# One load of the recurrence's weights for both sequences, and one turn of the output weights' sign

## The chip, the cores and the metric

The kernel runs on one core of one Trainium2 chip. Its engines are TensorE (PE, matrix products; PEld is its loading of weights), VectorE (DVE), ScalarE (ACT), GpSimd (POOL) and SyncE (SP), which here only issues transfers. The metric is the device time of one execution in microseconds. A profiled execution lies beside the timed ones.

## The reference, cut to what matters

Four layers are computed for two sequences of 512 tokens and 256 channels (attention and experts, a state space with a spline MLP, a linear recurrence with a table MLP, attention and experts). The change touches the third. Its first half is a linear recurrent unit with 32 complex states, kept as 64 real rows (real parts, then imaginary parts):

```
u_t  = B x_t                       B: 64 x 256, real rows and imaginary rows
h_t  = lambda * h_(t-1) + gamma * u_t      complex, by state
y_t  = C_re Re(h_t) - C_im Im(h_t) + D * x_t
```

The minus sign is why the imaginary half of the output weights is turned. The second half is a gated MLP whose weights come from a table of 16 values. Its products are independent of the recurrence, and both are added to the sequence.

## The kernel before, in words

Every layer is a block in which each engine runs its own list of instructions, and the blocks are separated by a barrier of all engines (`run`). One block holds one layer for one sequence. In the recurrence's blocks the sequences are worked on one after the other, sequence 0 and then sequence 1; `linear_recurrence(m, b, ..., split_here)` writes the lists, and `split_here` is true for sequence 0 only.

At the start of a block SP issues three transfers (L2597 to L2599): the input weights `w_b`, the output weights `w_c` and the skip weights `skip`. TensorE clears its accumulators with two small products (L2560, `clear_acc`), waits for `w_b` and `w_c`, and projects the normed input `xnT` by four products into a PSUM bank (L2605). VectorE waits for the loads and the projection, turns the sign of the lower half of `w_c` (L2648), and scales the projection into `h` (L2649). The recurrence over 512 tokens is then done by nine doublings: TensorE multiplies a shifted `h` by a power of lambda (L2612), VectorE adds the product to `h` (L2655). The first doubling stands ahead of the first table product; the other eight stand between the table MLP's items. The MLP's products go through a helper (L225). At the end `h` is multiplied by `w_c` into the accumulators (L2640).

For sequence 0 only, ScalarE rounds the table weights in three pieces (L2673) and GpSimd subtracts to get the low parts (L2692); TensorE waits for the first piece ahead of the first table product, for the second (the down weights) at item 1, and for the third ahead of item 4 of eight. In both sequences GpSimd then waits for `skip`, multiplies it by the normed input (`extra`, L2696) and adds that to the sequence (L2699). The join at the end of the block (L2729) adds the accumulators to the sequence, after GpSimd's two steps. The norm of the other sequence runs inside the block as well, in eight phases spread over the items (lines 588 to 659), and must not write `xn` before `extra` was made.

Of the kernel before, what the change touches and what calls it, by code (L numbers as in the profile page):

```python
# [28 lines left out]
FP32 = mybir.dt.float32  # L29
# [4 lines left out]
ALU = mybir.AluOpType  # L34
AXIS = mybir.AxisListType

P = 128
BATCH, T, D = 2, 512, 256
NT = T // P
# [2523 lines left out]

def linear_recurrence(m, b, ctx, parts, norm, split_here):

# [7 lines left out]
    sb = m.local(ctx)  # L2573
    w_b, w_c = sb("w_b", [P, KD, N2]), sb("w_c", [N2, D])
    h = sb("h", [N2, T])
# [3 lines left out]
    piece_high, piece_split = m.sig("lut_high"), m.sig("lut_split")  # L2579
    extra, skip = sb("extra", [P, NT, D]), sb("skip", [P, D])  # L2580
    skip_loaded, skip_step = m.sig("skip_loaded"), m.sig("skip_step")
# [14 lines left out]
    def sync(sp):  # L2596
        sp.dma_start(w_b[:], dram["lru_b"]).then_inc(loaded.sem, 16)  # L2597
        sp.dma_start(w_c[:], dram["lru_c"]).then_inc(loaded.sem, 16)
        sp.dma_start(skip[:], dram["lru_d"].broadcast_to([P, D])).then_inc(skip_loaded.sem, 16)  # L2599

    def tensor(pe):
        clear_acc(m, pe)
        pe.wait_ge(loaded.sem, loaded.at(32))
        for k in range(KD):
# [39 lines left out]
    def vector(dve):  # L2644
        dve.wait_ge(loaded.sem, loaded.at(32))
        dve.wait_ge(projected.sem, projected.at(1))

        nc.vector.tensor_scalar(w_c[STATES:], w_c[STATES:], -1.0, None, ALU.mult)  # L2648
        nc.vector.tensor_scalar(h[:], lru_psum, m.lru_gamma[:], None, ALU.mult).then_inc(h_ready.sem, 1)  # L2649

        def double(s):
            dve.wait_ge(h_ready.sem, h_ready.at(s + 1))
            dve.wait_ge(stepped.sem, stepped.at(s + 1))
            shift = 1 << s
            nc.vector.tensor_tensor(h[:, shift:], h[:, shift:], lru_psum[:, shift:], ALU.add)\  # L2655
              .then_inc(h_ready.sem, 1)

        double(0)
        gate(dve, 0, None, 0, 0)
        for n in range(ITEMS):  # L2660
            if n < NT:
                double(2 * n + 1)
                double(2 * n + 2)
            if n + 1 < ITEMS:
                gate(dve, n + 1, None, (n + 1) % NT, (n + 1) % 2)
            store_low(dve, n, n % 2)
            for phase in norm_phases(n):
                norm.vector(dve, phase)
# [18 lines left out]
    def gpsimd(pool):  # L2687
# [6 lines left out]

        pool.wait_ge(skip_loaded.sem, skip_loaded.at(16))
        nc.gpsimd.tensor_tensor(extra[:], m.xn[:], skip[:].unsqueeze(1).broadcast_to([P, NT, D]), ALU.mult)\  # L2696
# [4 lines left out]
    def close():  # L2701
        mlp.close()
        norm.close()
        if split_here:
            piece_high.close(3)
            piece_split.close(3)
        loaded.close(32)
        skip_loaded.close(16)
        skip_step.close(2)
        for s, n in ((projected, 1), (h_ready, STEPS + 1), (stepped, STEPS)):  # L2710
            s.close(n)
# [61 lines left out]
def hybrid_stack_kernel(nc, dram, out):  # L2773
    with ExitStack() as ctx:
# [32 lines left out]
        with ExitStack() as late_ctx:  # L2807
            m.hold_parts(late_ctx)
            with ExitStack() as parts_ctx:
                parts = [parts_ctx.enter_context(nc.sbuf_tensor(f"lut_{part}", [P, LUT_COLS], FP32R))  # L2810
                         for part in ("high", "low")]
                for b in range(BATCH):
                    with ExitStack() as layer_ctx:
                        m.turn_to(b)
                        skip_step = m.sig("skip_step")
                        norm = Norm(m, 1 - b, 2 + b, (5, 5), (skip_step.sem, skip_step.at(1)))
                        recurrence, done = linear_recurrence(m, b, layer_ctx, parts, norm, b == 0)
                        run(m, recurrence, join(m, b, done, (skip_step, 2)))
# [151 lines left out]
```

## Time and profile before

| what | us |
|---|---|
| median of 3 runs | 1654.25 |
| their range | 1653.96 to 1656.31 |
| the profiled execution | 1653.79 |
| its span, first to last instruction | 1651.9 |
| TensorE busy | 1528.8 (93%) |
| VectorE busy | 1148.0 (69%) |
| ScalarE busy | 952.4 (58%) |
| GpSimd busy | 703.5 (43%) |

Times in the rows are microseconds from the span's start unless ns is written. The mean granted clock of TensorE in the profiled execution is 0.979 of full speed. The recurrence's two blocks lie at about 977.9 to 1031.4 (sequence 0) and 1031.4 to 1080.8 (sequence 1). An idle time in square brackets stands before the instruction that ended it, with what released it.

### The profile page before, as it was taken

What the parts mean: (1) busy time and instruction counts of PE and PEld (TensorE: products, weight loads), DVE (VectorE), ACT (ScalarE), POOL (GpSimd) and SP (SyncE); (2) the same over time, 40 slices, a digit from 0 to 9 for tenths busy, and PEclk for the clock granted to TensorE, in tenths of its full rate; (3) what the DMA queues carried; (4) which work ended last, traced back from release to release, by engine and by line L of the source; (5) the groups of instructions that cost most, each with busy time, mean ns of one, the idle gap of its engine ahead of it and who ended that gap; (6) DMA issues with size and microseconds to landing.
All of it is one profiled execution on the core that took longest, in us unless ns stands there. A gap on an engine that the chain in (4) does not pass through costs nothing. (4 is left out here: it accounts for less than half of the span.)

```text
span 1651.9 us, 26447 instructions
## 1 busy us (share of the span) xinstructions
PE 1528.8 (93%) x8400; PEld 1208.0 (73%) x8400; DVE 1148.0 (69%) x2620; ACT 952.4 (58%) x2076; POOL 703.5 (43%) x686
## 2 busy tenths in 40 slices
PE   5999989979999998899989989879999997999998
PEld 4777779957787998555635547668888885888887
DVE  5887866558888667799889964446666444666733
ACT  5767656846666566666476533246666444665643
POOL 4999953323222233099639860121223222212222
PEclk9999999989999999999999999979999998999999
DMA  4212222111112121240050000011121112112121
GB/s 124 90 54 81 76 97 96 37 56 36 51 41 93 65 96 58 55 179 1 1 202 32 0 7 1 7 52 50 35 89 39 58 38 72 42 51 73 39 73 36
DMA packets 34334, 98.38 MB, mean 60 GB/s; under 512 B 6388, under 2 KB 11256, under 8 KB 32072
## 3 DMA queue, kind: packets, MB, share of 16 engines
q1 hardware_dynamic: 33064, 90.95, 16.5%
q0 software_dynamic: 1184, 6.37, 1.1%
q8 instruction: 44, 0.72, 0.2%
q14 instruction: 42, 0.34, 0.1%
HBM read 96.12 MB, written 1.18 MB: 59 GB/s over the span
## 5 line engine op out<-in xcount | busy, mean ns | idle before, releaser
L921 POOL TENSOR_TENSOR head_low<-head,head_high 128x512 fp32r<-128x512 f32 x64 | 81.6, 1276 | 453.3 <-ACT head_high L911 452.5
L1953 POOL TENSOR_TENSOR experts_low<-experts,experts_high 128x1024 fp32r<-128x1024 f32 (+3 forms) x62 | 138.9, 2243 | 256.5 <-ACT experts_high L1904 93.2
L2508 POOL TENSOR_TENSOR rings<-du,bc_rows 128x512 f32<-128x512 f32 x124 | 155.6, 1276 | 21.3 <-DMA bc_rows<-bc_rows 14.7
L1309 ACT ACTIVATE probs<-banks,neg_max 128x512 f32<-128x512 f32 (+3 forms) x256 | 133.6, 525 | 53.2 <-DVE neg_max L1192 47.7
L2434 DVE TENSOR_TENSOR_SCAN banks<-banks,rings 128x512 f32<-128x512 f32 x128 | 155.9, 1219 | 3.3 <-POOL rings L2508 2.3
L1586 DVE SCALAR_TENSOR_TENSOR hidden<-banks,weight,act_out 128x96 f32<-128x96 f32 (+1 forms) x192 | 62.7, 367 | 124.2 <-ACT act_out L1554 124.1
L1554 ACT ACTIVATE act_out<-banks 128x256 f32<-128x256 f32 (+2 forms) x112 | 47.4, 423 | 164.9 <-PE banks L225 164.7
L2226 PE MATMUL banks<-rings,ident 128*128 128x512 f32 x256 | 126.4, 607 | 16.6 <-DVE rings L2457 16.3
L225 PE MATMUL banks<-experts_high,xnT_high 128*128 128x384 f32 (+1 forms) x384 | 139.1, 362 | 0.8 <-PEq L187 0.8
L225 PE MATMUL banks<-xnT_high,head_high 128*128 128x512 f32 x256 | 109.9, 429 | 30.1 <-POOL head_low L921 23.5
L225 PE MATMUL banks<-experts_high,xnT_low 128*128 128x384 f32 (+1 forms) x384 | 137.2, 357 | 0.0
L225 PE MATMUL banks<-experts_low,xnT_high 128*128 128x384 f32 (+1 forms) x384 | 137.1, 357 | 0.0
L2332 ACT ACTIVATE banks<-delta,A 128x512 f32<-128x512 f32 x128 | 88.5, 692 | 72.3 <-DVE rings L2457 72.2
L1212 DVE TENSOR_REDUCE row_max<-banks 128x1 f32<-128x512 f32 (+3 forms) x256 | 117.4, 484 | 6.4 <-PE banks L1020 6.1
L1324 ACT ACTIVATE probsT<-banks 128x384 f32<-128x384 f32 (+3 forms) x192 | 87.4, 528 | 47.8 <-PE banks L1029 47.6
L225 PE MATMUL banks<-xnT_low,head_high 128*128 128x512 f32 x256 | 103.7, 405 | 0.0
L225 PE MATMUL banks<-xnT_high,head_low 128*128 128x512 f32 x256 | 103.5, 404 | 0.0
L1205 DVE TENSOR_SCALAR probs<-probs,row_inv 128x512 f32<-128x512 f32 (+3 forms) x240 | 98.1, 448 | 4.8 <-DVE row_inv L1198 0.3
L1162 DVE TENSOR_TENSOR w_in<-banks,w_in 32x512 f32<-32x512 f32 x128 | 87.2, 681 | 13.2 <-DMA w_in<-in_rope_sin 9.1
L2226 PEld LDWEIGHTS banks<-rings,ident 128*128 128x128 f32 x256 | 45.3, 191 | 68.2 <-DVE rings L2457 38.2
L1029 PE MATMUL banks<-ident,probs 128*128 128x128 f32 x640 | 82.2, 276 | 12.5 <-DVE probs L1205 12.3
L2457 DVE TENSOR_TENSOR rings<-banks,bc_rows 128x512 f32<-128x512 f32 x128 | 85.9, 672 | 0.0
(305 smaller groups left out, 4699.1 us busy)
## 6 DMA issues: line engine op xcount, KB each, us to landing
head<-in_heads SPq DMA_DIRECT2D x64, 384.0 KB, 3.1
experts<-in_experts SPq DMA_DIRECT2D x16, 1152.0 KB, 5.2
bc_rows<-bc_rows SPq DMA_DIRECT2D x30, 512.0 KB, 5.8
experts<-in_experts SPq DMA_DIRECT2D x16, 768.0 KB, 4.3
values<-in_values SPq DMA_DIRECT2D x32, 256.0 KB, 3.2
coef<-in_spline_coef POOLq DMA_DIRECT2D x8, 768.0 KB, 4.7
idx<-in_lut_idx SPq DMA_DIRECT2D x16, 134.0 KB, 2.1
x<-in_x SPq DMA_DIRECT2D x2, 512.0 KB, 4.5
```

Of the source, the lines that this page charges most:

```text
L225: last = nc.tensor.matmul(out, left[a], right[b], start=start and n == 0, stop=stop and n == 2, **kw)
L1162: chain.link(nc.vector.tensor_tensor(rot[to:to + 32, which], qk_psum[of:of + 32, which], rope_sin[of:of + 32], ALU.mult))
L1205: last = nc.vector.tensor_scalar(prob_tile(i), prob_tile(i), row_inv[:, i:i + 1], None, ALU.mult)
L1212: last = nc.vector.reduce_max(row_max[:, i:i + 1], score_tile(i), AXIS.X)
L1309: last = nc.scalar.activation(prob_tile(i), score_tile(i), ACT.Exp, bias=neg_max[:, i:i + 1], scale=QK_SCALE, accum_out=row_sum[:, i:i + 1])
L1324: nc.scalar.activation(probsT[:, at:at + cols], m.banks[:, k, 0:cols], ACT.Copy)\
L1953: nc.gpsimd.tensor_tensor(parts[gpar][1][:, columns], raw[gpar][:, columns], parts[gpar][0][:, columns].bitcast(FP32), ALU.subtract)\
L2226: nc.tensor.matmul(y_psum(c), m.ident[:], product[:, step % PRODUCTS], start=n == 0, stop=n == NS - 1)\
L2332: nc.scalar.activation(state_psum(step), delta[:, c], ACT.Exp, scale=A[:, c, n:n + 1])\
L2434: nc.vector.tensor_tensor_scan(state_psum(step), state_psum(step), inflow[:, step % INFLOWS], 0.0, ALU.mult, ALU.add).then_inc(scanned.sem, 1)
L2457: nc.vector.tensor_tensor(product[:, step % PRODUCTS], state_psum(step), C_of(n), ALU.mult)\
L2508: nc.gpsimd.tensor_tensor(inflow[:, step % INFLOWS], du[:, c], B_of(n), ALU.mult)\
```

## The change

The three weights become tiles that live over both blocks. Their transfers, TensorE's wait for them, GpSimd's wait for `skip`, and the turn of the sign are made for sequence 0 only. In sequence 0 the turn moves ahead of VectorE's wait for the projection.

```diff
-def linear_recurrence(m, b, ctx, parts, norm, split_here):
+def linear_recurrence(m, b, ctx, parts, weights, norm, split_here):
...
-    w_b, w_c = sb("w_b", [P, KD, N2]), sb("w_c", [N2, D])
+    w_b, w_c, skip = weights
...
-    extra, skip = sb("extra", [P, NT, D]), sb("skip", [P, D])
+    extra = sb("extra", [P, NT, D])
...
     def sync(sp):
-        sp.dma_start(w_b[:], dram["lru_b"]).then_inc(loaded.sem, 16)
-        sp.dma_start(w_c[:], dram["lru_c"]).then_inc(loaded.sem, 16)
-        sp.dma_start(skip[:], dram["lru_d"].broadcast_to([P, D])).then_inc(skip_loaded.sem, 16)
+        if split_here:
+            sp.dma_start(w_b[:], dram["lru_b"]).then_inc(loaded.sem, 16)
+            sp.dma_start(w_c[:], dram["lru_c"]).then_inc(loaded.sem, 16)
+            sp.dma_start(skip[:], dram["lru_d"].broadcast_to([P, D])).then_inc(skip_loaded.sem, 16)
 
     def tensor(pe):
         clear_acc(m, pe)
-        pe.wait_ge(loaded.sem, loaded.at(32))
+        if split_here:
+            pe.wait_ge(loaded.sem, loaded.at(32))
...
     def vector(dve):
-        dve.wait_ge(loaded.sem, loaded.at(32))
+        if split_here:
+
+            dve.wait_ge(loaded.sem, loaded.at(32))
+            nc.vector.tensor_scalar(w_c[STATES:], w_c[STATES:], -1.0, None, ALU.mult)
         dve.wait_ge(projected.sem, projected.at(1))
-
-        nc.vector.tensor_scalar(w_c[STATES:], w_c[STATES:], -1.0, None, ALU.mult)
         nc.vector.tensor_scalar(h[:], lru_psum, m.lru_gamma[:], None, ALU.mult).then_inc(h_ready.sem, 1)
...
-        pool.wait_ge(skip_loaded.sem, skip_loaded.at(16))
+        if split_here:
+            pool.wait_ge(skip_loaded.sem, skip_loaded.at(16))
...
-        loaded.close(32)
-        skip_loaded.close(16)
+            loaded.close(32)
+            skip_loaded.close(16)
...
+                weights = [parts_ctx.enter_context(nc.sbuf_tensor(f"lru_{name}", shape, FP32))
+                           for name, shape in (("b", [P, KD, 2 * STATES]), ("c", [2 * STATES, D]), ("skip", [P, D]))]
```

## Rows read from the trace of the kernel before

**Rows 1.** The page, part 1, and the granted clock in 40 slices of part 2

```profile
PE 1528.8 (93%) x8400; PEld 1208.0 (73%) x8400; DVE 1148.0 (69%) x2620; ACT 952.4 (58%) x2076; POOL 703.5 (43%) x686
...
PEclk9999999989999999999999999979999998999999
```

**Rows 2.** Windows: length, busy time (instructions) by engine, clock, DMA share, GB/s

```profile
977.90:1031.40 53.50, 46.18 (x232) 32.76 (x232) 23.21 (x57) 17.76 (x35) 14.30 (x5) 0.90 0.02 6
1031.40:1080.80 49.40, 43.25 (x232) 31.01 (x232) 22.29 (x61) 12.51 (x31) 4.75 (x2) 0.97 0.02 6
```

**Rows 3.** Waits from 977.9 to 1080: total us, times, longest

```profile
PE banks L2612 <- DVE h L2649: 4.6, 2, 3.1
...
PE banks L2605 <- DMA w_c<-in_lru_c: 3.9, 2, 2.0
```

**Rows 4.** Order in time on GpSimd: start, duration, instruction, idle before

```profile
979.39 3.10 POOL L2692 TENSOR_TENSOR lut_low<-lut_w,lut_high 128x1376 fp32r<-128x1376 f32 x1 [13.69 <-ACT lut_high L2673]
...
979.39 6.48 POOL L2692 TENSOR_TENSOR lut_low<-lut_w,lut_high 128x1376 fp32r<-128x1376 f32 x2 [13.69 <-ACT lut_high L2673]
...
1035.53 2.40 POOL L2696 TENSOR_TENSOR extra<-xn,skip 128x1024 f32<-128x1024 f32 x1 [41.76 <-DMA skip<-in_lru_d]
```

**Rows 5.** Order in time on TensorE, start of sequence 1

```profile
1031.48 0.59 PE L2560 MATMUL acc<-mask_bf,ident_bf 1*128 1x512 bf16 x2 [1.64 <-PEq L187]
1034.05 3.32 PE L2605 MATMUL banks<-xnT,w_b 128*64 128x512 f32 x4 [1.98 <-DMA w_c<-in_lru_c]
1038.88 1.07 PE L2612 MATMUL banks<-h,lru_step 64*64 64x511 f32 x2 [1.51 <-DVE h L2649]
...
1042.96 0.43 PE L225 MATMUL banks<-lut_high,xnT_high 128*128 128x344 f32 x1
```

**Rows 6.** Order in time on VectorE, start of sequence 1

```profile
1037.48 0.59 DVE L2648 TENSOR_SCALAR w_c<-w_c 32x256 f32<-32x256 f32 x1 [6.32 <-PE banks L2605]
1038.09 0.74 DVE L2649 TENSOR_SCALAR h<-banks,lru_gamma 64x512 f32<-64x512 f32 x1
```

**Rows 7.** Windows of 1 us; the clock is the third number from the end

```profile
987.00:988.00 1.00, 1.00 (x2) 0.12 (x2) 0.00 (x0) 0.00 (x0) 1.00 (x1) 0.50 0.00 0
...
994.00:995.00 1.00, 1.00 (x8) 1.00 (x8) 0.68 (x1) 0.00 (x0) 0.00 (x0) 1.00 0.00 0
...
1034.00:1035.00 1.00, 0.95 (x2) 0.42 (x3) 0.00 (x0) 0.00 (x0) 0.00 (x0) 0.72 0.28 92
1035.00:1036.00 1.00, 1.00 (x2) 0.23 (x1) 0.00 (x0) 0.00 (x0) 0.47 (x1) 0.50 0.02 7
...
1038.00:1039.00 1.00, 0.12 (x1) 0.12 (x2) 0.81 (x2) 0.00 (x0) 0.99 (x1) 1.00 0.00 0
```

**Rows 8.** Order in time on TensorE: four fp32 products of another stage

```profile
847.62 1.12 PE L2137 MATMUL banks<-xmT,w_in 128*128 128x512 f32 x2 [0.20 <-DVE delta L2413]
848.58 1.02 PE L2137 MATMUL banks<-xn,w_in 128*128 128x512 f32 x2
```

**Rows 9.** Order in time on TensorE, start of sequence 0

```profile
980.50 3.27 PE L2605 MATMUL banks<-xnT,w_b 128*64 128x512 f32 x4 [1.92 <-DMA w_c<-in_lru_c]
986.84 1.96 PE L2612 MATMUL banks<-h,lru_step 64*64 64x511 f32 x2 [3.07 <-DVE h L2649]
...
993.95 0.43 PE L225 MATMUL banks<-lut_high,xnT_high 128*128 128x344 f32 x1
```

**Rows 10.** Order in time on VectorE, start of sequence 0

```profile
983.88 2.14 DVE L2648 TENSOR_SCALAR w_c<-w_c 32x256 f32<-32x256 f32 x1 [6.21 <-PE banks L2605]
986.04 0.74 DVE L2649 TENSOR_SCALAR h<-banks,lru_gamma 64x512 f32<-64x512 f32 x1
```

**Rows 11.** Instructions on the tile `h`: duration ns min/median/max, first and last start

```profile
L2655 DVE TENSOR_TENSOR h<-h,banks x18: 411/661/679, 988.9 to 1062.7; 64x511 f32<-64x511 f32 x2, 64x510 f32<-64x510 f32 x2, 64x508 f32<-64x508 f32 x2, 64x504 f32<-64x504 f32 x2
```

**Rows 12.** Windows of 1 us in the attention stage; the three between show 0.50

```profile
1095.00:1096.00 1.00, 1.00 (x6) 0.56 (x5) 0.00 (x0) 0.00 (x0) 0.00 (x0) 0.94 0.00 0
...
1099.00:1100.00 1.00, 1.00 (x7) 0.73 (x7) 1.00 (x5) 0.97 (x1) 0.00 (x0) 0.85 0.00 0
```

More of the change, by code:

```diff
@@ L2816, in hybrid_stack_kernel @@
                         norm = Norm(m, 1 - b, 2 + b, (5, 5), (skip_step.sem, skip_step.at(1)))
-                        recurrence, done = linear_recurrence(m, b, layer_ctx, parts, norm, b == 0)
+                        recurrence, done = linear_recurrence(m, b, layer_ctx, parts, weights, norm, b == 0)
                         run(m, recurrence, join(m, b, done, (skip_step, 2)))
```

## The prediction, made before the changed kernel was built

> **What bounds the kernel now.** TensorE is busy for 93% of the span, so I read its stalls first and ask of every other engine only whether TensorE waits for it [rows 1]. The whole-kernel chain of waits is of little use here: it is followed back from the end and never reaches the recurrence. So I took the two stages of the recurrence by themselves. The window view gives 53.50 us for sequence 0 and 49.40 us for sequence 1, at a mean granted clock of 0.90 and 0.97, where the page's row of the clock shows 9s but for three slices [rows 1, 2]. Both stages run the same products on TensorE (232 each), so the reader should already ask why one is 4 us longer and why the clock is low in both. The view of waits between 977.9 and 1080 names what belongs to the change: TensorE waits 3.9 us in two pieces for the transfer of `w_c` (the projection, L2605), and 4.6 us in two pieces for `h` (L2612 after L2649) [rows 3]. GpSimd waits 41.76 us for `skip`, across most of a stage, but nobody waits for GpSimd there [rows 4]. The rest comes from the order in time on TensorE, VectorE and GpSimd at the start of each stage, and from the granted clock microsecond by microsecond.
>
> **Sequence 1, the transfers.** TensorE issues the two small products that clear the accumulators at 1031.48; they end at 1032.07. The projection starts at 1034.05, with 1.98 us of idle time ended by the DMA of `w_c` [rows 5]. The change takes out the three transfers and the wait, and its input `xnT` was finished in the stage before, so the four products can follow the two directly: 1.98 us, all of it on the path, since everything after hangs on the projection. On SP nothing is queued behind the three issues in this stage, so their removal there is worth nothing by itself.
>
> **Sequence 1, the sign.** The projection ends at 1034.05 + 3.32 = 1037.37. VectorE turns the sign of `w_c` from 1037.48 and starts `h` at 1038.09; without the turn `h` can start at 1037.48: 0.61 us, on the path, for TensorE's first doubling waits for `h` [rows 5, 6].
>
> **Sequence 1, the clock.** The four projection products take 3.32 us here [rows 5]. The granted clock tells why: it is 0.72 in the microsecond from 1034 and 0.50 in the one from 1035, that is 1.2 instead of 2.4 GHz, and full again from 1038 [rows 7]. Between 1029.84, the end of the last stage's products (the start at 1031.48 less its idle 1.64), and 1034.05 TensorE had done nothing but the 0.59 us pair. Four products of 128x512 in fp32 at the full clock take 1.98 us in another stage, from 847.62 to 848.58 + 1.02 = 849.60 [rows 8]. If the transfer's gap goes, the projection starts after 1.64 us of idle and the pair, about 0.1 us of overlap aside, and I expect it to run and end before any drop: 3.32 - 1.98 = 1.34 us. The bound on one side is 0 (the drop comes all the same; it can't cost more, since it is there now), on the other 1.34. I take 1.34, since the gap that precedes the drop is cut from 3.62 us of idle in 4.21 to 1.64 in 2.23. Sum for sequence 1: 1.98 + 0.61 + 1.34 = 3.93 us.
>
> **Sequence 0, the sign.** Here the transfers stay, and TensorE's wait for them (1.92 us) stays too [rows 9]. But the turn moves ahead of VectorE's wait for the projection. Before, it starts at 983.88, the projection having ended at 980.50 + 3.27 = 983.77, and takes 2.14 us for 32x256 elements, against 0.59 us in sequence 1; `h` starts at 986.04 [rows 6, 10]. What is different is GpSimd. Its first two subtractions of table weights run from 979.39 to 982.49 and on to 985.87; the turn that started inside the second ends 986.02, that is 0.15 us after it. In sequence 1 GpSimd's `extra` ends at 1035.53 + 2.40 = 1037.93 and the turn at 1038.07, again 0.14 after it [rows 4, 6, 10]. So the turn is held to the end of the GpSimd instruction that it meets, and alone costs some 0.15 us. After the change VectorE can turn when `w_c` has landed, about 980.50, inside GpSimd's first piece; it should end at 982.49 + 0.15 = 982.64, which is 1.13 us before the projection's end. `h` then starts at 983.88: 2.16 us, on the path. The cover is that 1.13 us; if it were gone, the turn would show again on VectorE ahead of `h`. The wait that moves has only the turn queued behind it, and TensorE's own wait for the same 32 already ends no earlier.
>
> The Trainium skill, SBUF — State Buffer, "Who interferes with whom", says that a VectorE instruction in a two-port mode and a GpSimd instruction exclude each other for a whole instruction, whichever comes second being blocked. By that rule the turn ends behind the first piece, and the trace agrees (2.14 us against 0.59 us for the same work) [rows 6, 10].
>
> **Sequence 0, the clock.** TensorE does nothing from 983.77 to 986.84, 3.07 us, and the granted clock is 0.50 in the microsecond from 987 and full again only from 994 [rows 7, 9]. In sequence 1 the same gap is 1.51 us (1037.37 to 1038.88) and the clock stays full behind it [rows 5, 7]. After the change the gap is 1.51 - 0.61 = 0.90 us in both. The price is read from the same instructions at both clocks: from the first doubling, over twelve table products and the second doubling, to the next table product it is 993.95 - 986.84 = 7.11 us here and 1042.96 - 1038.88 = 4.08 us in sequence 1. The difference is 3.03 us [rows 5, 9]. Bounds 0 and 3.03; I take 3.03, since the new gap is shorter than the one that did no harm. Sum for sequence 0: 2.16 + 3.03 = 5.19 us.
>
> **What comes late next.** In sequence 0 the first doubling ends at 986.84 + 1.96 = 988.80; moved by 2.16 and run at the full clock (1.0 us instead of 1.96) it lets the first table product start near 985.7, which needs GpSimd's first piece, ready at 982.49; the down weights (985.87) are wanted behind the third table product and the last piece (985.87 + 3.1, about 989) ahead of the fifth, both later than that even when moved. GpSimd's use of `skip` in sequence 1 moves from 1035.53 to the start of the stage, about 1031.5, and nobody waits [rows 4]; held back again it would still cost nothing, for it is used at the join only. The VectorE additions into `h`, which now run beside other GpSimd work than before, took 0.661 us in the median and 0.679 at most over both stages, so none of them was held up [rows 11]. The same 9.12 us therefore passes on to the stages that follow, which hang on these through a barrier of all engines. The three tiles kept longer are memory, not time: 0, by bounds 0 and 0.
>
> **The sum.** 5.19 + 3.93 = 9.12 us. The profiled execution took 1653.79 us (span 1651.9), 0.46 under the median of 1654.25; from the median, 1654.25 - 9.12 = 1645.13. I forecast 1645.1.
>
> **The rivals.**
> A. The clock does not come back. The transfers and the turn leave the path as above, but a low stretch still falls on the first products of one or both sequences, or falls in a later stage instead. For it: the clock also fell near 1095.9 while TensorE was busy for the whole of that microsecond, so idle time isn't all of it [rows 12]. Against: the new gaps are shorter than the 1.51 us that did nothing. With none of the clock's gain the change is worth 2.16 + 1.98 + 0.61 = 4.75, giving 1649.5; with only the sequence 1 term lost, 1646.5; with only sequence 0's lost, 1648.2. Chance 0.25.
> The Trainium skill, TensorE: Matmul & The Clock Gate, Part 1, says that the monitor's window runs free of the kernel's start, so that the point of a change varies from run to run. By that rule the moment of each drop against the work is a matter of chance, which is rival A; the one trace shown can't tell.
> B. The turn loses its race and is held to the end of GpSimd's second piece (985.87) as now. Then `h` in sequence 0 starts at 986.04, the gap of 3.07 us and the low clock stay, and only 3.93 remains: 1650.3. For it: GpSimd's pieces follow each other without a gap [rows 4]. Against: before, the turn got in at the seam between second and third. Chance 0.05.
> C. The three transfers were hidden anyway: something else holds the projection of sequence 1 to 1034.05. For it: the DMA is only the last that ended. Against: GpSimd's wait of 41.76 us ends with a transfer of the same three [rows 4], and the projection has no other fresh input. Then 5.19 + 0.61 = 5.80, giving 1648.5. Chance 0.04.
> D. Slower. In the attention stage behind, the clock fell near 1095.9 with TensorE busy, for five rows (0.94, three of 0.50, 0.85), which costs 0.06 + 1.50 + 0.15 = 1.71 us of full clock [rows 12]. That dense stage and its twin start 9 us earlier after the change, and the moments of such drops could fall on more of their work. The change is slower than before from six additional ones (10.3 us against 9.12), and by over 0.2% (3.3 us) from eight: 1645.1 + 13.7 = 1658.8. Against: the page's row of the clock shows 9s in all slices of those stages but two [rows 1]. Chance 0.02.
>
> **How the numbers follow.** Forecast 0.64, A 0.25, B 0.05, C 0.04, D 0.02. The range reaches up to A's and nearly B's time, 1650.0, and down to where the low clock under sequence 0's projection goes as well (3.27 - 1.98 = 1.29) and one stretch like D's less in a later stage (1.71): 1645.1 - 3.0 = 1642.1; I take 1642.0. A measurement of this kernel can tell about 0.2%, 3.3 us, from no change, so "same" is 1650.9 to 1657.6. The forecast and rivals B and C lie below it, narrowly for B; giving half of B and a seventh of A to "same" by scatter of the runs makes 0.06. Faster 0.92, same 0.06, slower 0.02.
>
> **What would show it.** In the profile after: one issue each of `w_b`, `w_c` and `skip`; the projection of sequence 1 directly behind the clearing pair, idle near 0, four products in about 2.0 us; the turn once, starting near 980.5 and ended by 982.7, before the projection ends; `h` in sequence 0 starting 0.1 us behind the projection and TensorE's gap there 0.9 us; the granted clock 1.00 through both doublings and the first table products. Stage lengths should be near 48.3 and 45.5 us. The prediction is wrong if the turn ends after 983.8, if the clock is 0.50 in either place, or if the attention stage behind takes more low clock than before.

## The result, and the profile after

The changed kernel takes 1645.15 us in the median of 20 runs (1640.40 to 1653.06), the kernel before 1654.11 us in the median of 20 runs beside it (1649.08 to 1663.19). The ratio is 0.9945 with a 95% interval of 0.9931 to 0.9958: faster by 0.55%, some 9 us, which is clear of the 0.2% that can be told. The profiled execution took 1643.16 us with a span of 1641.6. By the interval the gain is between 6.9 and 11.4 us. Single executions of either kernel lie over 12 us apart, so one profile of each says where a wait went, and the means over the runs say how much it was worth.

The page, beside [rows 1], and the windows of the two sequences, beside [rows 2]:

```profile
PE 1524.4 (93%) x8400; PEld 1205.3 (73%) x8400; DVE 1148.1 (70%) x2619; ACT 952.4 (58%) x2076; POOL 703.1 (43%) x686
...
PEclk9999999989999999999999999989999998999999
```

```profile
976.20:1024.70 48.50, 43.45 (x232) 30.96 (x232) 23.22 (x57) 17.76 (x35) 14.34 (x5) 0.96 0.02 6
1024.70:1073.20 48.50, 44.51 (x232) 32.33 (x232) 21.75 (x60) 12.52 (x31) 4.72 (x2) 0.93 0.00 1
```

The first window is the whole of sequence 0: from clearing product to clearing product it is 1024.76 - 976.22 = 48.54 us, where it was 53.49 before. The clock rose there from 0.90 to 0.96. In sequence 1 it fell from 0.97 to 0.93, and the gain of that sequence is small in this one execution. Sequence 1 is best measured from its clearing product to the attention's first product. These are the first clearing product and the attention's first product of the kernel before, and then of the changed kernel:

```profile
977.99 0.59 PE L2560 MATMUL acc<-mask_bf,ident_bf 1*128 1x512 bf16 x2 [1.64 <-PEq L187]
1086.41 0.80 PE L225 MATMUL banks<-xnT_high,head_high 128*128 128x512 f32 x1 [6.89 <-POOL head_low L921]
976.22 0.59 PE L2560 MATMUL acc<-mask_bf,ident_bf 1*128 1x512 bf16 x2 [1.64 <-PEq L187]
1078.34 0.80 PE L225 MATMUL banks<-xnT_high,head_high 128*128 128x512 f32 x1 [6.94 <-POOL head_low L921]
```

With the clearing products of sequence 1 at 1031.48 and 1024.76, sequence 1 took 54.93 us before and takes 53.58 us here: 1.35 us less, where the sum has 3.93.

TensorE's order in time, sequence 0 and then sequence 1 (start, duration, instruction, idle before), which answers to [rows 9] and [rows 5]:

```profile
978.75 3.58 PE L2607 MATMUL banks<-xnT,lru_b 128*64 128x512 f32 x4 [1.93 <-DMA lru_c<-in_lru_c]
983.16 1.07 PE L2614 MATMUL banks<-h,lru_step 64*64 64x511 f32 x2 [0.84 <-DVE h L2652]
987.23 0.42 PE L225 MATMUL banks<-lut_high,xnT_high 128*128 128x344 f32 x1
...
1024.76 0.59 PE L2560 MATMUL acc<-mask_bf,ident_bf 1*128 1x512 bf16 x2 [1.65 <-PEq L187]
1025.28 2.35 PE L2607 MATMUL banks<-xnT,lru_b 128*64 128x512 f32 x4
1028.46 1.96 PE L2614 MATMUL banks<-h,lru_step 64*64 64x511 f32 x2 [0.84 <-DVE h L2652]
...
1034.84 0.43 PE L225 MATMUL banks<-lut_high,xnT_high 128*128 128x344 f32 x1
```

The gap ahead of the first doubling is 0.84 us in both, down from 3.07 and 1.51. The projection of sequence 1 follows the clearing pair (the two small products that clear the accumulators) without a gap. From the first doubling to the first table product behind the second one, sequence 0 takes 987.23 - 983.16 = 4.07 us, where it took 7.11; sequence 1 takes 1034.84 - 1028.46 = 6.38, where it took 4.08. VectorE and GpSimd, beside [rows 10], [rows 6] and [rows 4]:

```profile
978.73 2.15 DVE L2650 TENSOR_SCALAR lru_c<-lru_c 32x256 f32<-32x256 f32 x1 [2.82 <-DMA lru_c<-in_lru_c]
982.37 0.74 DVE L2652 TENSOR_SCALAR h<-banks,lru_gamma 64x512 f32<-64x512 f32 x1 [1.49 <-PE banks L2607]
...
1027.66 0.74 DVE L2652 TENSOR_SCALAR h<-banks,lru_gamma 64x512 f32<-64x512 f32 x1 [3.22 <-PE banks L2607]
```

```profile
977.63 3.10 POOL L2695 TENSOR_TENSOR lut_low<-lut_w,lut_high 128x1376 fp32r<-128x1376 f32 x1 [13.69 <-ACT lut_high L2676]
...
1024.74 2.38 POOL L2700 TENSOR_TENSOR extra<-xn,lru_skip 128x1024 f32<-128x1024 f32 x1 [32.70 <-SPq L187]
```

The turn still takes 2.15 us, but it starts when the weights land, ends at 980.88, which is 0.15 us behind GpSimd's first piece (980.73), and lies wholly under the projection. GpSimd uses `skip` at the very start of sequence 1. The clock in single microseconds, beside [rows 7]:

```profile
982.00:983.00 1.00, 0.33 (x1) 0.00 (x0) 0.64 (x1) 0.00 (x0) 1.00 (x1) 0.85 0.00 0
983.00:984.00 1.00, 0.84 (x2) 0.19 (x2) 0.11 (x1) 0.00 (x0) 1.00 (x1) 1.00 0.00 0
...
1028.00:1029.00 1.00, 0.54 (x1) 0.29 (x2) 0.41 (x1) 0.00 (x0) 1.00 (x1) 0.50 0.00 0
```

In sequence 0 the clock is full from the first doubling on, as forecast. In sequence 1 it went to half during the projection, 1.9 us after TensorE had taken up work, and stayed there for 6.8 us (1026.7 to 1033.5), over the first doubling and most of the twelve table products.

### The profile page after: what moved, and what is told of

The parts are those of the page before. It is cut to its first block and busy times, and to the rows that moved or that the text cites. A ratio compares the mean times of both kernels' runs of the same rounds, so it can differ in the third digit from the quotient of the medians.

```text
span 1641.6 us, 26441 instructions
## 1 busy us (share of the span) xinstructions
PE 1524.4 (93%) x8400; PEld 1205.3 (73%) x8400; DVE 1148.1 (70%) x2619; ACT 952.4 (58%) x2076; POOL 703.1 (43%) x686
```

## The experiments

Two theories stood against each other. The first is the sum of the prediction: a path of 4.75 us (waiting, turning) and a clock that the shorter gaps give back. The rival says that the clock's drops fall where they will, so that only the path is earned. A second question is what held the turn for 2.14 us.

**The changed kernel again, each part alone, and GpSimd out of the way.** Four kernels on one chip; the kernel before took 1656.53 us there (29 runs).

The changed kernel unedited:

> The changed kernel itself, as the yardstick of the three others on this chip. By my sum it is 9.1 us faster than the kernel before (a ratio of 0.9945). In its trace the turn of the sign ends near 0.15 us behind GpSimd's first subtraction, and TensorE's gap ahead of the first doubling is 0.84 us in both sequences. The rival that takes the clock for a matter of chance expects the two low stretches of the recurrence at other places than in the first trace after the change (979 to 982 and 1026 to 1033), and a time anywhere from 1640 to 1653.

Measured: 1647.06 us (6 runs), ratio 0.9932 (0.9909 to 0.9955). The turn, the gap of 0.84 us and the 48.32 us of sequence 0 came back. Sequence 1 met a low stretch of 13.7 us (1025.7 to 1039.3). TensorE's first two doublings there, and the clock beside them:

```profile
1028.34 1.96 PE L2614 MATMUL banks<-h,lru_step 64*64 64x511 f32 x2 [0.84 <-DVE h L2652]
1033.97 1.96 PE L2614 MATMUL banks<-h,lru_step 64*64 64x510 f32 x2
```

```profile
1030.00:1031.00 1.00, 1.00 (x4) 0.77 (x4) 0.59 (x1) 0.00 (x0) 0.00 (x0) 0.50 0.00 0
1039.00:1040.00 1.00, 1.00 (x5) 0.41 (x3) 0.00 (x0) 0.40 (x1) 0.00 (x0) 0.84 0.00 0
```

Both doublings take 1.96 us, the mark of the half clock, and TensorE is busy for the whole of the microseconds shown. Sequence 1 takes 58.16 us in this profile, 3.2 us more than before the change, 1.5 us of it a longer wait for GpSimd's first step of the attention (8.41 us against 6.89 before). So the short gap does not protect the sequence in every execution.

Loads once, the turn of sequence 0 left in its old place (against the changed kernel):

```diff
             dve.wait_ge(loaded.sem, loaded.at(32))
+        dve.wait_ge(projected.sem, projected.at(1))
+        if split_here:
             nc.vector.tensor_scalar(w_c[STATES:], w_c[STATES:], -1.0, None, ALU.mult)
-        dve.wait_ge(projected.sem, projected.at(1))
```

> The transfers and waits of sequence 1 are gone and the sign is turned once, but in sequence 0 the turn stays behind VectorE's wait for the projection. My sum: only sequence 1's 3.93 us are left (1.98 of waiting, 0.61 of turning, up to 1.34 of clock), so 1650.2, 5.2 us slower than the changed kernel. In the trace the turn of sequence 0 takes about 2.1 us and ends 0.15 us behind GpSimd's second subtraction; TensorE's gap there is 3.07 us. If the clock's part of sequence 0 is not real, it is only 2.2 us slower than the changed kernel.

Measured: 1649.73 us (12 runs), ratio 0.9964 (0.9946 to 0.9982), 6.0 us faster than before (3.0 to 8.9 by the interval), where the sum has 3.93. The turn and TensorE at the start of both sequences:

```profile
984.76 1.90 DVE L2652 TENSOR_SCALAR lru_c<-lru_c 32x256 f32<-32x256 f32 x1 [6.46 <-PE banks L2607]
...
987.48 1.27 PE L2614 MATMUL banks<-h,lru_step 64*64 64x511 f32 x2 [2.82 <-DVE h L2653]
...
1031.16 1.93 PE L2607 MATMUL banks<-xnT,lru_b 128*64 128x512 f32 x4
1033.92 1.07 PE L2614 MATMUL banks<-h,lru_step 64*64 64x511 f32 x2 [0.84 <-DVE h L2653]
```

The turn ends at 986.66; GpSimd's second piece ended at 986.52, 0.14 us before. Sequence 1 is what I had predicted for it: the projection takes 1.93 us at the full clock, and the stretch from its clearing pair to the attention's first product is 50.84 us, where it was 1086.41 - 1031.48 = 54.93 before. That is 4.09 us against 3.93 in the sum.

The turn moved in sequence 0, all else as before (against the kernel before):

```diff
-        dve.wait_ge(projected.sem, projected.at(1))
-
-        nc.vector.tensor_scalar(w_c[STATES:], w_c[STATES:], -1.0, None, ALU.mult)
+        if split_here:
+            nc.vector.tensor_scalar(w_c[STATES:], w_c[STATES:], -1.0, None, ALU.mult)
+        dve.wait_ge(projected.sem, projected.at(1))
+        if not split_here:
+            nc.vector.tensor_scalar(w_c[STATES:], w_c[STATES:], -1.0, None, ALU.mult)
```

> The kernel before with one line moved: in sequence 0 the turn stands ahead of the wait for the projection. Transfers, waits and the second turn stay in sequence 1. My sum: 5.19 us faster than before (2.16 of path and 3.03 of clock), 1649.1. Without the clock's part 2.2 us faster, 1652.1. In the trace the gap of TensorE ahead of the first doubling is about 0.85 us in sequence 0 and 1.51 us in sequence 1.

Measured: 1651.96 us (12 runs), ratio 0.9970 (0.9954 to 0.9987), 5.0 us faster than before (2.2 to 7.6 by the interval), against 5.19 in the sum and 2.2 without the clock, which lies at the very edge of the interval: the times alone do not exclude it. In this profile sequence 0 takes 48.28 us, 5.21 less than before, with a gap of 0.84 us. In sequence 1 the gap is 1.35 us, and the low clock lasted 10.2 us there instead of 3.4. The two parts alone give 0.36% and 0.30%, together 0.66%, and the whole change on the same chip 0.68%: they add, as far as intervals of that width can tell.

GpSimd held back while VectorE turns, the turn itself unmoved (against the kernel before):

```diff
             at = slice(*pieces[piece])
-
+            if n == 1:
+                pool.wait_ge(h_ready.sem, h_ready.at(1))
...
+        pool.wait_ge(h_ready.sem, h_ready.at(1))
         pool.wait_ge(skip_loaded.sem, skip_loaded.at(16))
```

> The kernel before with the turn where it was, but GpSimd waits for h ahead of its second subtraction in sequence 0 and ahead of the use of skip in sequence 1, so that it is idle while VectorE turns the sign. If the turn is held only by the GpSimd instruction that it meets, it takes some 0.15 to 0.3 us in both sequences instead of 2.14 and 0.59, h starts 2.0 and 0.4 us earlier, and the kernel is 2.4 to 5.4 us faster than before (the upper end with the clock's 3.03 us of sequence 0). If GpSimd has nothing to do with it, the turn takes 2.14 and 0.59 us as before and the time is that of before.

Measured: 1652.25 us (12 runs), ratio 0.9970 (0.9952 to 0.9989), 5.0 us faster than before. The turn in sequence 0 and in sequence 1:

```profile
984.23 0.28 DVE L2648 TENSOR_SCALAR w_c<-w_c 32x256 f32<-32x256 f32 x1 [6.48 <-PE banks L2605]
...
1034.85 0.28 DVE L2648 TENSOR_SCALAR w_c<-w_c 32x256 f32<-32x256 f32 x1 [7.72 <-PE banks L2605]
```

With no GpSimd instruction running it takes 0.28 us in both places, against 2.14 and 0.59 before. So 1.86 and 0.31 us of it were waiting for GpSimd. TensorE's gap ahead of the first doubling is 1.21 us in both sequences, and the clock is full behind it. This is the experiment that settles the turn: the same instruction at the same place, and only GpSimd moved. The Trainium skill, SBUF — State Buffer, "Who interferes with whom", calls this an exclusive lock for the whole instruction; the runs agree, with ends 0.14 to 0.15 us behind GpSimd's.

**What else could be earned, and what the terms hang on.** Four kernels on another chip, where the kernel before took 1657.46 us (16 runs).

A step of the turn's size back in sequence 1, in front of `h` (this edit and the next three are against the changed kernel):

```diff
         dve.wait_ge(projected.sem, projected.at(1))
+        if not split_here:
+            nc.vector.tensor_scalar(w_c[STATES:], w_c[STATES:], 1.0, None, ALU.mult)
```

> The changed kernel with a second step on the output weights in sequence 1, a multiplication by 1.0 of the same 32x256 elements behind the wait for the projection, where the turn stood. Nothing holds GpSimd back any more, so its addition to x now runs from about 1027.2 to 1029.6 of the first trace after the change, and the step would begin at 1027.66 inside it. If VectorE is held to the end of the GpSimd instruction that it meets, the step takes 1.9 to 2.1 us instead of the 0.59 us of before, and the kernel is about 2 us slower than the changed kernel, more by a low clock. If 0.6 us is what the step costs, it is 0.6 us slower.

Measured: 1648.80 us (11 runs), ratio 0.9948 (0.9929 to 0.9967). In the profile the expected collision was missed: the low clock made the projection longer (3.67 us), so the step came late enough to meet only the last 0.10 us of GpSimd's addition.

```profile
1032.70 0.28 DVE L2653 TENSOR_SCALAR lru_c<-lru_c 32x256 f32<-32x256 f32 x1 [4.97 <-PE banks L2607]
```

GpSimd's addition ran from 1030.46 for 2.34 us to 1032.80, and the step was over at 1032.98. What this step costs depends on the clock of another engine, for that decides which GpSimd instruction it meets. The runs say more than the one profile. What their spans would be at the full clock (worked out as in the table further down) is 2.8 us less than for the kernel before beside them, where the changed kernel has 4.8 us less. The step therefore costs 2.0 us in the mean, plus or minus 1.4, which is what was expected of the long hold; a price of 0.6 us lies at the edge. The low clock of this profile also covered the start of sequence 0, from 976.5 to 990.2, although TensorE's gap is 0.84 us there as well:

```profile
983.30 1.96 PE L2614 MATMUL banks<-h,lru_step 64*64 64x511 f32 x2 [0.84 <-DVE h L2654]
```

The first table products ahead of the first doubling:

```diff
-        double(0)
-
         if split_here:
             pe.wait_ge(piece_split.sem, piece_split.at(1))
         multiply(0, 0, 0)
+        double(0)
```

> The changed kernel with the first twelve table products ahead of the first doubling instead of behind it. TensorE then works while VectorE makes h, and the gap of 0.84 us is gone in both sequences. I expect 1.7 us from the two gaps and up to 3 us more where a low stretch of the clock began behind such a gap; the rival that takes the doublings for the path expects no gain, since each of them then comes 1 us later against the items.

Measured: 1645.40 us (6 runs), ratio 0.9927 (0.9903 to 0.9952). With the changed kernel's 0.9932 on the other chip this is no gain that can be told. The profile says why: the gap only moved, to the second doubling.

```profile
1034.98 1.06 PE L2614 MATMUL banks<-h,lru_step 64*64 64x510 f32 x2 [0.84 <-DVE h L2657]
```

From the clearing pair to the attention it takes 50.79 us at a full clock, against 50.84 with the doubling first. The rival of that expectation was right: the doublings are the path, and TensorE's gap is wherever the first two meet.

The three transfers in the block before, into the memory of the spline's weights once those are no longer needed (which is why the rows below name `spline_gu` for the recurrence's weights):

```diff
+    def sync(sp):
+        sp.wait_ge(multiplied.sem, multiplied.at(items))
+        sp.dma_start(w_b[:], m.dram["lru_b"]).then_inc(loaded.sem, 16)
+        sp.dma_start(w_c[:], m.dram["lru_c"]).then_inc(loaded.sem, 16)
+        sp.dma_start(skip[:], m.dram["lru_d"].broadcast_to([P, D])).then_inc(skip_loaded.sem, 16)
...
-                    run(m, scan, join(m, b, done))
+                    run(m, scan, join(m, b, done), *((recurrence_ahead(m, weights),) if b else ()))
```

> The changed kernel with the three transfers issued in the block before, once the spline's weights are dead, into their place. TensorE's wait of 1.93 us at the start of sequence 0 goes, and the sign is turned before GpSimd's first subtraction begins. I expect 1.9 us, and about 1.3 to 1.6 us more from the projection of sequence 0 at the full clock: 3.2 to 3.5 us faster than the changed kernel. If the clock falls by chance and not behind the gaps, 1.9 us.

Measured: 1647.26 us (6 runs), ratio 0.9938 (0.9913 to 0.9963): no gain that can be told. The wait of 1.93 us did go, and the projection ran at 1.93 us. Sequence 0 takes 46.62 us, only 1.7 to 1.9 less than the changed kernel's, because another wait took the place. VectorE, GpSimd and TensorE in sequence 0:

```profile
976.55 0.28 DVE L2644 TENSOR_SCALAR spline_gu<-spline_gu 32x256 f32<-32x256 f32 x1 [0.32 <-PEq L187]
...
990.84 1.58 DVE L600 TENSOR_SCALAR rs<-mv 128x4 f32<-128x4 f32 x1
```

```profile
990.02 2.37 POOL L2697 TENSOR_TENSOR x<-x,extra 128x1024 f32<-128x1024 f32 x1
```

```profile
993.05 1.04 PE L2608 MATMUL banks<-h,lru_step 64*64 64x496 f32 x2 [1.72 <-DVE h L2652]
```

The turn, ahead of all GpSimd work, takes 0.28 us. But the norm's small step L600, four elements a row, now falls into GpSimd's addition to `x` and is held to its end (992.39): 1.58 us, where the changed kernel has 0.17. The addition into `h` is queued behind it, and TensorE waits 1.72 us instead of 0.32. The covers of a sum have to be looked up again when the work under them moves: GpSimd's list starts at the block's start, VectorE's had come 2 to 3 us nearer to it.

Both together:

```diff
-        double(0)
...
+        double(0)
...
+                    run(m, scan, join(m, b, done), *((recurrence_ahead(m, weights),) if b else ()))
```

> Both of the last two together. If the gains add, 5 to 7 us faster than the changed kernel, near 1639. What could take the place of the waits is GpSimd's first subtraction in sequence 0: it ends 4.5 us behind the block's start, and the projection would now end 2.4 us behind it, so the first table product would wait about 2 us for it. Then in sequence 0 only the doubling's order is lost and the sum is 2 us less than the two gains.

Measured: 1645.90 us (6 runs), ratio 0.9927 (0.9903 to 0.9952). No gain over either of the two alone can be told, and the 1639 expected if they add is missed. The named wait is there, 2.13 us for GpSimd's first piece:

```profile
982.04 0.43 PE L225 MATMUL banks<-lut_high,xnT_high 128*128 128x344 f32 x1 [2.13 <-POOL lut_low L2688]
```

In this profile a low stretch of 10.2 us begins 1.0 us behind that wait (983.1 to 993.3), and sequence 0 takes 51.37 us.

**The clock, and the best version.** Four kernels on a third chip; the kernel before took 1655.75 us there (27 runs).

TensorE kept busy in the waits by products that are overwritten, first in the kernel before:

```diff
+        for _ in range(4):
+            nc.tensor.matmul(lru_psum, m.ident[:, 0:N2], m.xnT[:, 0], start=True, stop=True)
         pe.wait_ge(loaded.sem, loaded.at(32))
...
         last.then_inc(projected.sem, 1)
+        for _ in range(5 if split_here else 2):
+            nc.tensor.matmul(m.banks[0:N2, 4, :], m.ident[:, 0:N2], m.xnT[:, 0], start=True, stop=True)
```

> The kernel before, with TensorE kept busy in the recurrence's waits by products whose results are overwritten: four of 64x512 ahead of the wait for the loads, and behind the projection five in sequence 0 and two in sequence 1. They lie inside waits, 0.43 us each at the full clock (1.7 us in a wait of 1.9, 2.2 in one of 3.07, 0.9 in one of 1.51). If idle time in these places is what lowers the clock, the low stretches at the start of both sequences are mostly gone: the stretch from the first clearing product to the attention's first product shrinks from 108.4 us towards 104 (3.03 and 1.34 less), and the time by some 4 us. If the drops fall where they will, the time stays within noise of the kernel before, or is up to 3 us longer, since at the low clock the added products no longer fit into the waits.

Measured: 1651.70 us (12 runs), ratio 0.9976 (0.9957 to 0.9994), 4 us faster than before (1.0 to 7.1 by the interval), although the filling was too long for the waits. I had taken an instruction for a product: the profile records a product of 512 columns in fp32 as two instructions of 0.43 us each, so that four of them are eight (and the projection is two products, shown as x4, and not the four that the text ahead of the prediction says).

```profile
976.28 3.65 PE L2604 MATMUL banks<-xnT,ident 128*64 128x512 f32 x8
979.77 1.88 PE L2607 MATMUL banks<-xnT,w_b 128*64 128x512 f32 x4
981.49 4.45 PE L2610 MATMUL banks<-xnT,ident 128*64 128x512 f32 x10
985.87 1.07 PE L2616 MATMUL banks<-h,lru_step 64*64 64x511 f32 x2
```

The first doubling starts 985.87 - 975.77 = 10.10 us behind the clearing pair, 1.25 us later than before (986.84 - 977.99 = 8.85). In sequence 1 it is 7.53 against 7.40. Yet the window of the start of sequence 0 shows a clock of 1.00, and so does that of sequence 1:

```profile
975.80:990.00 14.20, 14.20 (x41) 5.29 (x41) 3.94 (x4) 5.65 (x5) 12.75 (x5) 1.00 0.06 18
1027.50:1042.00 14.50, 14.50 (x48) 6.48 (x48) 3.24 (x5) 0.91 (x2) 4.72 (x2) 1.00 0.07 19
```

The other half of the expectation was missed. The stretch from the first clearing product to the attention's first product takes 1084.13 - 975.77 = 108.36 us in this profile and did not shrink towards 104. Sequence 0 is 1.8 us shorter, the 3.03 us of the clock less the 1.25 us of too long filling. Sequence 1 is 1.7 us longer, nearly all of it a longer wait of TensorE for GpSimd ahead of the attention (8.50 us against 6.89). Where the rest of the 4 us came from, this profile doesn't show.

The changed kernel filled in the same way has four such products in sequence 0 only and one behind each projection:

```diff
+            for _ in range(4):
+                nc.tensor.matmul(lru_psum, m.ident[:, 0:N2], m.xnT[:, 0], start=True, stop=True)
             pe.wait_ge(loaded.sem, loaded.at(32))
...
+        for _ in range(1 if split_here else 1):
+            nc.tensor.matmul(m.banks[0:N2, 4, :], m.ident[:, 0:N2], m.xnT[:, 0], start=True, stop=True)
```

> The changed kernel with the same filling: four products ahead of the one wait for loads that is left, one behind each projection, in the gap of 0.84 us. Against the filled kernel before it should show the path alone, 2.16 + 1.98 + 0.61 = 4.75 us, if both keep their clock. Against the changed kernel it gains 1.3 us or more by a full clock under the first projection, if idle time lowers it, and nothing otherwise.

Measured: 1644.84 us (12 runs), ratio 0.9929 (0.9908 to 0.9950). Against the filled kernel before the ratio is 0.9929 / 0.9976 = 0.9953, 7.8 us by the ratios and 6.9 by the medians. That is more than the 4.75 us of path, because the filling costs the kernel before more of its path than the changed one. In the two traces the first doubling comes 10.10 - (982.55 - 975.84) = 3.39 us earlier in sequence 0 and 7.53 - (1027.45 - 1024.16) = 4.24 us earlier in sequence 1, 7.6 us together, which agrees with the times. The comparison therefore does not measure the unfilled path; it shows the clock full at the start of both sequences in both profiles. Against the changed kernel unedited, which has 0.9945 beside it, the filled one is lower by 0.16%, some 2.6 us, but the two intervals overlap: the 1.3 us or more expected can't be told from nothing.

The transfers ahead as above, and GpSimd's addition to `x` behind the fourth addition into `h`, where semaphore `h_ready` stands at 5 (only the second edit is shown):

```diff
         pool.wait_ge(skip_step.sem, skip_step.at(1))
+        pool.wait_ge(h_ready.sem, h_ready.at(5))
         nc.gpsimd.tensor_tensor(m.x_of[b][:], m.x_of[b][:], extra[:], ALU.add).then_inc(skip_step.sem, 1)
```

> The changed kernel with the three transfers in the block before, as in the run of load_ahead, and with GpSimd's addition to x waiting for the fourth addition into h. In the run of load_ahead a small VectorE step of the norm (L600) met GpSimd's addition and took 1.58 us instead of 0.17, and TensorE waited 1.72 instead of 0.31 us behind it. If the exclusion is the cause, that step is back at 0.17 us and the stage of sequence 0 is 45.2 us, 3.2 us shorter than the changed kernel's 48.4. If the cause is another, the stage stays at 46.6 us.

Measured: 1641.49 us (6 runs, 1635.56 to 1641.99), ratio 0.9901 (0.9872 to 0.9930), the fastest kernel of this case; the changed kernel beside it has 0.9945 (0.9923 to 0.9966). The norm's step is back at 0.17 us, and TensorE's wait behind it at 0.33:

```profile
993.25 0.17 DVE L600 TENSOR_SCALAR rs<-mv 128x4 f32<-128x4 f32 x1
```

```profile
994.15 2.37 POOL L2698 TENSOR_TENSOR x<-x,extra 128x1024 f32<-128x1024 f32 x1 [3.18 <-DVE h L2652]
```

Sequence 0 took 46.55 us in this profile and not the 45.2 expected, since its projection happened to run at the half clock (3.52 us instead of 1.93, 1.6 us). The exclusion as cause is confirmed by the step; the length of the stage missed by a low stretch.

And the changed kernel, unedited, for the third time:

> The changed kernel itself once more, as the yardstick on this chip. In its trace the path is as before it: the turn of the sign ended 0.15 us behind GpSimd's first subtraction, gaps of 0.84 us in both sequences. If the low clock's place is chance, its low stretches lie elsewhere than in the two profiles so far, and the stretch from the first clearing product to the attention's first lies between 99 us (no low clock) and 107 us.

Measured: 1646.80 us (10 runs), ratio 0.9945 (0.9923 to 0.9966). The stretch from the first clearing product to the attention's first takes 99.49 us here; in the first two profiles of the changed kernel it took 1078.34 - 976.22 = 102.12 and 106.48. The chain of work is the same in all three, but not every wait outside the change is: the one ahead of the attention is 6.94, 8.41 and 7.24 us. Without it the stretch is 95.18, 98.07 and 92.25 us, and 101.53 in the kernel before. So the three profiles gain 6.35, 3.46 and 9.28 us in the recurrence, where the sum has 9.12. Sequence 1 ran at the full clock this time:

```profile
1024.90:1073.00 48.10, 41.78 (x232) 30.79 (x232) 21.74 (x60) 12.52 (x31) 4.72 (x2) 0.99 0.03 9
```

**Path and clock by the means.** Each run has its span and its mean granted clock. Span times (1 - clock) is the time lost to the low clock if it were wholly busy time, which overstates it where TensorE is idle; the rest is what the span would be at the full clock. The means, worked out from the runs:

```
kernel (chips)              runs   mean us   mean clock   lost us   rest us
before (the 3 chips)          72   1656.7    0.9768       38.5      1616.1
changed (and the result's)    36   1646.7    0.9798       33.2      1611.3
before, filled                12   1652.3    0.9829       28.2      1622.3
changed, filled               12   1644.4    0.9828       28.2      1614.5
ahead, GpSimd yields           6   1640.6    0.9822       29.2      1609.5
```

The change takes 4.8 us off the rest and 5.2 us off what is lost to the clock, with 95% intervals of plus or minus 0.8 and 1.5 from the scatter of the runs. The sum had 4.75 and 4.37. For the two parts, each against the kernel before on its chip, the loads alone take 2.0 (plus or minus 1.2) off the rest and 4.0 (2.9) off the loss, where the sum has 2.59 and 1.34; the early turn takes 2.1 (1.3) and 2.6 (2.0), where it has 2.16 and 3.03. So the clock's share is shown for the whole change, and its division between the sequences isn't.

The split is rough, as the filled kernel before shows. Its rest is 6.2 us longer, of which the traces account for 4.0: the first doublings start 1.25 and 0.13 us later, and the 1.29 and 1.34 us that the low clock cost the projections before are no longer there to be taken off.

## Why the prediction was right

Forecast 1645.1, measured 1645.15. The agreement to 0.05 us is luck: the interval of the gain is 4.5 us wide, and the mean of the 20 runs is 1646.6. The path terms are right for their reasons, shown one by one; the clock's terms stand only in the mean over runs. By the prediction's own signs it was wrong in one place: the clock was to be full at the start of both sequences, and in the profile of the result it was 0.50 in sequence 1.

- *The transfers of sequence 1 (1.98 us).* Right: the projection follows the clearing pair at once, in every profile of a kernel without them. Rival C (hidden anyway) is refuted.
- *The sign in sequence 1 (0.61 us).* Right: gap 0.84 us instead of 1.51, 0.67 less. Half of the turn was waiting for GpSimd: 0.28 us alone.
- *The sign in sequence 0 (2.16 us).* Right, shown from two sides: moving the turn and holding GpSimd back each free the path, and each gives 5.0 us. The turn ended 0.15 us behind the first piece, as worked out; the cover is 982.33 (projection's end) less 980.88, 1.45 us in this profile. Rival B did not happen in any profile with the early turn. One small step was wrong: the turn alone takes 0.28 us and not 0.15. The 0.15 is only the part behind GpSimd's end.
- *The clock in sequence 0 (3.03 us).* Right in size: 7.11 us became 4.07. The part alone gave 5.0 us where the path without the clock is 2.2, and the intervals of both ways of doing it reach just down to that or to less (2.2 and 1.8). Eight profiles have a gap of 0.84 or 1.21 us ahead of the first doubling of sequence 0, with the table products behind it. In seven the clock is full from the first doubling through the second. In the eighth, that of the kernel with the added step, the low clock covered all of the start of sequence 0. So the term is earned in most of these executions and not in all.
- *The clock in sequence 1 (1.34 us).* This is the term that was too sure. Rival A happened there in two of the three profiles of the changed kernel, over 6.8 and 13.7 us; with the loads alone and in the third profile the term was earned whole. Over all nine profiles in which the projection follows the clearing pair, the filled kernel aside, the low clock fell on the projection in five and not in four. In the three profiles with the transfers still in sequence 1 (before, the turn moved, GpSimd held back) it fell there each time. The step that was too sure is "I expect it to run and end before any drop". That a shorter idle stretch makes a drop rarer is borne out by the means, and by the filled kernel before: a mean clock of 0.983 against 0.977, and 4 us less with more work in it. That the place of a drop is chance fits the three profiles of one kernel, with 95.18, 98.07 and 92.25 us over the same instructions once the wait ahead of the attention is taken off. The Trainium skill, TensorE: Matmul & The Clock Gate, Part 1, says of this that the window runs free of the kernel. The three profiles fit that, and no run here tests it. Forecast and rival A were therefore not exclusive: the gain of the clock is a mean over runs, 5.2 us, and I had priced it as if each execution had it.
- *The stage lengths.* 48.54, 48.32, 48.28 and 48.33 us for sequence 0 in the three profiles of the changed kernel and the one with only the turn moved, against 48.3; in the kernel with the added step, whose sequence 0 is the same, the low clock made it 51.90. For sequence 1 the forecast was 3.93 us less than before. Measured to the attention's first product, it is 1.35 us less, 3.23 us more and 3.77 us less in the three profiles of the changed kernel, and 4.09 less with the loads alone.
- *Slower (D).* Not seen in the times. The 1651.9 - 1641.6 = 10.3 us between the spans of the two profiled executions are 108.42 - 102.12 = 6.30 us from the first clearing product to the attention, 977.99 - 976.22 = 1.77 ahead of it, where nothing was changed, and the rest behind it. It would have been wrong to credit the change with what lies ahead of it.

What stays open is what brings the clock down where TensorE is busy ([rows 12], and the 13.7 us of the second profile). No run here was made to tell that.

## What to carry to other kernels

Look at short waits of TensorE for what they do to the clock behind them: here 4.8 us of path brought some 5 us of clock with it, but as a mean over runs, so judge by many runs and use one profile only for who waits for whom. A small VectorE step that takes several times longer than its size asks for may have met a GpSimd instruction, as the three looked at here had; move either out of the other's way, and when work is moved, look up again what each such step will now meet. Read off a row how many instructions one product is recorded as before filling a gap with it.

## What the runs showed of the hardware that was not expected

- A VectorE step of 128x4 elements took 1.58 us instead of 0.17 beside a GpSimd addition: the size of the step has no part in the delay, only what is left of the GpSimd instruction.
- Executions of the changed kernel lie 12.7 us apart (1640.40 to 1653.06); the mean clock of a run goes with it (0.984 in the fastest of the 20, 0.976 in the slowest).
- The half clock lasted 13.7 us with TensorE busy for the whole of most microseconds (second profile of the changed kernel, 1025.7 to 1039.3), and it began 1.5 us after TensorE had taken up work.
- More work in the waits made this kernel faster: the filled kernel before has 15 more products in its two blocks and runs 4 us shorter.
